# Score tiles in two PSUM slots, probability tiles in a slot of their own, and the order of the work in a step

## What the kernel computes

```python
k_eff = (W_dq.T @ W_uq.T @ W_uk).reshape(nh, hs, n_kvl)
v_eff = jnp.transpose((W_uv.T @ W_o.T).reshape(n_kvl, nh, hs), (1, 0, 2))
c_kv = x @ W_dkv.T
q = (x @ W_dq.T @ W_uq.T).reshape(B, T, nh, hs)
q_lat = jnp.einsum('bqhd,hdl->bhql', q, k_eff)
attn = jnp.einsum('bhql,bkl->bhqk', q_lat, c_kv) / sqrt(hs)
attn = jax.nn.softmax(jnp.where(causal[None, None], attn, -jnp.inf), axis=-1)
y = jnp.einsum('bhql,hld->bqhd', jnp.einsum('bhqk,bkl->bhql', attn, c_kv), v_eff)
x = _layernorm(x + y.reshape(B, T, C))
gate, up = fp4_linear(x, w_gate), fp4_linear(x, w_up)
x = _layernorm(x + fp4_linear(jax.nn.silu(gate) * up, w_down))
```

## Time and profile before

| | |
|---|---|
| median of 3 runs | 754.0 us (752.06 to 757.2) |
| profiled execution | 758.44 us, its span 756.6 us |
| PE busy | 563.6 us, 74% of the span |
| DVE busy | 532.3 us, 70% |
| ACT busy | 412.3 us, 54% |
| POOL busy | 316.0 us, 42% |
| granted TensorE clock, mean | 0.876 of full speed |

### The profile page before, as it was taken

One profiled execution on the slowest core, in us unless ns is written; L12 is line 12 of the kernel. 1 busy time (PEld: TensorE's weight loads), 2 busy tenths in 40 slices (PEclk: granted clock), 3 DMA queues, 4 the chain that ended last, 5 costly groups with the idle time before them and its releaser, 6 DMA issues.

```text
span 756.6 us, 15168 instructions
## 1 busy us (share of the span) xinstructions
PE 563.6 (74%) x5863; PEld 254.3 (34%) x5863; DVE 532.3 (70%) x981; ACT 412.3 (54%) x598; POOL 316.0 (42%) x441
## 2 busy tenths in 40 slices
PE   4275988589787888788888889696978897862623
PEld 2132333233333434333333334242323342421412
DVE  0389787388889767788788778888787784264461
ACT  2311766377665766565576666564656675742220
POOL 4520032000436654433337464533273536258682
PEclk9655999799998999999898999998899998995565
DMA  3393006602300192020300480203000000000000
GB/s 101 77 241 101 2 3 151 145 2 51 94 5 12 31 210 56 15 52 16 92 16 2 90 196 11 56 10 78 3 16 3 3 2 16 1 15 0 0 14 15
DMA packets 34222, 37.91 MB, mean 50 GB/s; under 512 B 6390, under 2 KB 19766, under 8 KB 34150
## 3 DMA queue, kind: packets, MB, share of 16 engines
q1 hardware_dynamic: 33238, 36.39, 20.0%
q10 hardware_dynamic: 912, 0.54, 0.3%
HBM read 19.64 MB, written 16.78 MB: 48 GB/s over the span
## 4 chain that ended last, share of the span: by engine, by line
PE 39%; DVE 31%; POOL 13%; issue 10%; ACT 4%; DMA 2%; SPq 1%; POOLq 0%; DVEq 0%; ACTq 0%
DVE top L837 19%; PE yt_ps L556 11%; PE ring L537 6%; PE ring L520 5%; PE misc L495 3%; PE ring L507 2%; PE misc L466 2%; POOL eg L1151 2%; POOL hx L1123 2%; POOL hx L1121 2%; POOL hx L1125 1%; DVE z L906 1%; PE misc L455 1%; PE misc L486 1%; DVE hc L963 1%
## 5 line engine op out<-in xcount | busy, mean ns | idle before, releaser
L837 DVE TENSOR_REDUCE top<-ring 128x2 f32<-128x1024 f32 (+3 forms) x384 | 349.6, 948 | 113.4 <-PE ring L507 80.2
L715 ACT ACTIVATE probs<-ring 128x1024 f32<-128x1024 f32 x288 | 293.8, 1027 | 132.1 <-PE ring L507 79.7
L556 PE MATMUL yt_ps<-probs,v_op 128*32 128x512 f32 (+3 forms) x1536 | 171.6, 520 | 0.5 <-ACT probs L715 0.5
L537 PE MATMUL ring<-q_op,k_op 59*128 59x512 bf16 (+3 forms) x768 | 124.0, 346 | 50.2 <-DVE top L837 40.3
L520 PE MATMUL ring<-k_op,q_op 56*128 56x512 f16 (+3 forms) x768 | 127.8, 355 | 44.5 <-ACT probs L715 18.9
L520 PEld LDWEIGHTS ring<-k_op,q_op 56*128 56x128 bf16 x768 | 38.4, 96 | 171.0 <-issue 116.8
L1144 POOL TENSOR_TENSOR r<-r,yq 128x128 f32<-128x128 f32 x32 | 14.6, 457 | 168.3 <-DVE yq L876 168.3
L537 PEld LDWEIGHTS ring<-q_op,k_op 59*128 59x128 f16 x768 | 37.7, 95 | 120.8 <-DVE top L837 58.7
L507 PE MATMUL ring<-ident,mask_s 64*128 64x64 bf16 x1024 | 59.5, 198 | 0.0
L507 PEld LDWEIGHTS ring<-ident,mask_s 64*128 64x128 bf16 x1024 | 47.7, 102 | 17.7 <-issue 5.0
L507 PEld LDWEIGHTS ring<-ident,mask_t 64*128 64x128 bf16 x1024 | 47.2, 100 | 18.2 <-issue 6.8
(11 more groups left out here) (170 smaller groups left out, 758.4 us busy)
## 6 DMA issues: line engine op xcount, KB each, us to landing
q_op<-scratch_q SPq DMA_DIRECT2D x32, 224.0 KB
k_op<-scratch_k SPq DMA_DIRECT2D x32, 224.0 KB
scratch_k<-k_part SPq DMA_DIRECT2D x32, 192.0 KB, 3.3
scratch_q<-q_part SPq DMA_DIRECT2D x32, 128.0 KB, 3.1
scratch_q<-q_part SPq DMA_DIRECT2D x16, 192.0 KB, 3.3
xp<-in_L_attn_x_dram SPq DMA_DIRECT2D x4, 512.0 KB, 4.4
r<-in_L_attn_x_dram SPq DMA_DIRECT2D x8, 256.0 KB, 2.8
out_dram<-z SPq DMA_DIRECT2D x8, 256.0 KB, 2.3
```

The lines of the kernel that those rows point to most:

```text
L537: last = nc.tensor.matmul(ring[slot][:, e, at:at + n], k_op[lo:lo + rows, pair, j * P:(j + 1) * P], q_op[lo:lo + rows, pair, (c + 1) * CHU ...
L556: last = nc.tensor.matmul(yt_ps[32 * q:32 * (q + 1), lo:CHUNK], v_op[:, j, 4 * a + q, :], probs[:, (STEPS * a + tile) % P_RING, q % 2, at: ...
L715: nc.scalar.activation(probs[:, n % P_RING, :, :], ring[(2 * n + 1) % 3][:, :, :], ACT.Exp, scale=SCALE).then_inc(t_exp.sem, 1)
L837: last = nc.vector.tensor_reduce(top[:, kc, :, p, i], ring[slot][:, :, at:at + n], AX.X, ALU.max)
```

## The change

Slots 0 and 1 now hold first-pass tiles alone, in turn, and slot 2 holds second-pass tiles alone, until the first-pass tiles run out in the last batch; from there the second pass uses all three. The waits follow: a first-pass tile waits for the maximum of the body two before, a second-pass tile for the exp of the step before. On TensorE the second-pass tile comes right behind the first-pass tile, and the jobs behind both; on ScalarE exp comes first in a step, ahead of the jobs' reads, the k parts and the sigmoid. The 24 tiles ahead of the loop use two slots.

```diff
@@ -317,6 +317,10 @@
 
         block = ctx.enter_context(nc.Block())
 
+        def probs_slot(m):
+
+            return 2 if m < B * BODY - STEPS - LEAD else m % 3
+
         def tile_pos(b, a, s):
 
             u = a + s // STEPS
@@ -578,9 +582,9 @@
                     nc.tensor.transpose(misc[0:w, 0:P], wd[:, f * P:f * P + w], ident[:, :]).then_inc(prep_mm.sem, 1)
 
             for s in range(STEPS + LEAD):
-                if s >= 3:
-                    pe.wait_ge(s_max.sem, s - 2)
-                score_max(0, s // STEPS, s % STEPS, s % 3)
+                if s >= 2:
+                    pe.wait_ge(s_max.sem, s - 1)
+                score_max(0, s // STEPS, s % STEPS, s % 2)
                 if 4 <= s < 4 + 3 * FT:
                     weight_t(s - 4)
                 if s == STEPS + 1:
@@ -598,23 +602,19 @@
                         a, s = n // STEPS, n % STEPS
                         nb, na, ns = tile_pos(b, a, s + STEPS + LEAD)
                         if nb < B:
-                            if n < 2 and b == 0:
-                                pe.wait_ge(s_max.sem, STEPS + LEAD)
-                            else:
-                                pn = b * BODY + n - 2
-                                pe.wait_ge(t_exp.sem, pn + 1)
-                            score_max(nb, na, ns, 2 * n % 3)
-                    for job in jobs_at(b, n):
-                        misc_job(*job)
+                            pe.wait_ge(s_max.sem, b * BODY + n + STEPS + LEAD - 1)
+                            score_max(nb, na, ns, n % 2)
                     if b < B:
 
                         if nb < B:
-                            pe.wait_ge(s_max.sem, b * BODY + n + STEPS + LEAD)
+                            if b * BODY + n > 0:
+                                pe.wait_ge(t_exp.sem, b * BODY + n)
                         else:
                             pe.wait_ge(s_max.sem, B * BODY)
                             pe.wait_ge(t_exp.sem, b * BODY + n - 2)
-                        score_probs(b, a, s, (2 * n + 1) % 3)
-
+                        score_probs(b, a, s, probs_slot(b * BODY + n))
+                    for job in jobs_at(b, n):
+                        misc_job(*job)
                     for w, at in enumerate(W_STEP):
                         g = n - at
                         if g % STEPS == 0 and g >= 0 and b < B:
@@ -712,7 +712,7 @@
                 if g >= 0:
 
                     act.wait_ge(av_mm.sem, g // STEPS * WS + FREED[g % STEPS])
-                nc.scalar.activation(probs[:, n % P_RING, :, :], ring[(2 * n + 1) % 3][:, :, :],
+                nc.scalar.activation(probs[:, n % P_RING, :, :], ring[probs_slot(b * BODY + n)][:, :, :],
                                      ACT.Exp, scale=SCALE).then_inc(t_exp.sem, 1)
 
             def sigmoid(b, t):
@@ -772,6 +772,8 @@
             for b in range(B + 1):
                 for n in range(BODY):
                     a, s = n // STEPS, n % STEPS
+                    if b < B:
+                        exps(b, a, s)
                     for job in jobs_at(b, n):
                         misc_read(*job)
                     if n in K_PART_AT and b + 1 < B:
@@ -779,9 +781,6 @@
                     if b > 0:
                         for stage, t in tile_at(b, n, H_A if b < B else TAIL_H_A):
                             sigmoid(b - 1, t)
-                    if b < B:
-                        exps(b, a, s)
-
                     if s == 7 and b < B:
                         out_copy(b, NC * a)
                     if s == 1:
@@ -859,7 +858,7 @@
             dve.wait_ge(wq_v.sem, 3)
             nc.vector.tensor_scalar(w_b[:, :, :], w_b[:, :, :], 1.0, ROUND, ALU.max, ALU.mult).then_inc(wq_v.sem, 1)
             for s in range(STEPS + LEAD):
-                maximum(0, s // STEPS, s % STEPS, s % 3)
+                maximum(0, s // STEPS, s % STEPS, s % 2)
                 if s == STEPS - 1:
                     combine(0, 0)
 
@@ -991,7 +990,7 @@
                     if b < B:
                         nb, na, ns = tile_pos(b, a, s + STEPS + LEAD)
                         if nb < B:
-                            maximum(nb, na, ns, 2 * n % 3)
+                            maximum(nb, na, ns, n % 2)
                             if ns == STEPS - 1:
                                 combine(nb, na)
                     for kind, jb, k in jobs_at(b, n):
```

## The result

The changed kernel takes **778.5 us** (median of 4 runs, 775.57 to 780.17), the kernel before, in the same session, 755.6 us (4 runs, 752.06 to 760.12). The ratio is 1.0299, 95% interval 1.0261 to 1.0337: 22.6 us slower, where +11 was forecast. The profiled execution took 780.17 us, span 778.2, mean granted clock 0.867; the one before 758.44, 756.6 and 0.876.

A forecast was written before the change was run, and what follows sets the result against it. TensorE was held back by T waiting for max (40.3 us) and S for exp (18.9). Batch terms 6.5 + 1.5 + 3.0 + 0 gave +11 us: 769 on the profiled execution, 765 against the 754.0 median; range 742 to 787.

The forecast's parts named there:

- Batch 0: +6.5: Batch 0: +2.4 us from T_0 to T_25, nothing in steps 25 to 35, +4.1 from T_36 to the end.
- "+1.5" for batch 1: Batch 1: same sum as batch 2's +3.0 us, half given back for one long wait for max before T_36.
- "-1.0" for steps 63 to 71: Batch 2, steps 63 to 71: VectorE full, TensorE gets a tile and its value matmuls ahead, gaining about 1.0 us.
- I take the loss of its first 48 steps and this gain as equal: Batch 3: first 48 steps' loss equals the last 24 steps' gain with three slots for T; sum 0.
- steps 25 to 35 neither gain nor lose: Batch 0, after the last q part is split: SP's queue sets 25.3 us whatever TensorE does; change 0.
- the second sigmoid chain gives 1.1 back: Batch 2, steps 36 to 53: a saving of 1.1 us at the second sigmoid chain, within a term of +1.1.
- T_18 is now ahead, which gives 1.0 back: Batch 2, steps 11 to 17: T_18 no longer behind the q job waiting for up_product; saves 1.0 us, term +0.7.
- +0.5: Batch 2, steps 0 to 10: TensorE's jobs fill most rounds; 24.5 us against 24.02 before.
- rival (1): The forecast: single slot's round binds in lean steps and outweighs what is freed; 765 us, own range 757 to 778, 50%.
- (2): Not slower: freeing T from waiting for max decides, where VectorE has long lists in batches 1 to 3; 736 us, 16%.
- (3): Losses and gains cancel: rounds overlap with work better, or stall chains give back more; 748 to 757 us, 28%.
- (4): TensorE's clock falls to 1.2 GHz in batch 0's lean quads from short idling; about 830 us, 6%.

The follow-up runs named there:

- the slots alone: Kernel before with only the changed slots and waits, its own order kept on TensorE and ScalarE: 779.4 us, ratio 1.0309.
- the short exp: Exp cut to 256 of 512 columns from step 6 of each batch: changed kernel 746.0 us, kernel before 752.1 us.
- batches 1 and 2 changed: Kernel before, its order kept, with the changed slots in batches 1 and 2 alone: 9.8 us slower (5.1 to 14.5).
- the order only: Kernel before with only the changed order on TensorE and ScalarE, three shared slots and waits kept: 763.4 us, ratio 1.0075.

## Why the prediction was off by half

**The mechanism was right.** A single slot closes the round T, exp, T at 1.50 us, and it binds: shown by the slots alone (+23.3) and by the short exp (31 us off the changed kernel, 4 off the other). The forms were right too: 1.50 to 1.51, 1.56 to 1.57 and 1.62 to 1.63 us in lean steps, 29.95 us for the quad where 30.4 was forecast and 27.20 stood before.

**What failed is the size of the sum.** "Batch 0: +6.5" measured 8.2 by itself, "+3.0 for batch 2" 4.3 and "0" for batch 3 2.6, each with the forecast inside its interval or at its edge. Batches 1 and 2 together, forecast at +4.5, measured 9.8 (5.1 to 14.5): that term is too low clear of the noise. "+1.5" for batch 1 is 5.5 as the difference of two kernels of one session; its place isn't shown, for in the trace of batches 1 and 2 changed, steps 11 to 62 of batch 1 took 118.59 us for 119.34. The terms are too low by 9.6 us together, and some 3 more (no more than the intervals allow) came with all batches changed. I counted losses and then set gains against them. These did not come, or were paid for elsewhere:

- "-1.0" for steps 63 to 71: TensorE did gain 3.2 us there, and paid 6.0 in the eleven steps behind, since VectorE's list has to be done first.
- "I take the loss of its first 48 steps and this gain as equal" for batch 3: steps 11 to 47 lost 3.8 us (84.46 for 80.63), and steps 48 to 70, with three slots for T, gained nothing (35.35 for 35.15).
- "steps 25 to 35 neither gain nor lose" in batch 0: SP's queue did hold them at its length (25.8 us from its first write at 121.74 to T_36, 25.3 before), but it starts later. With q's job and its read behind T and exp, the first write comes 2.9 us behind T_25, for 0.8 before, and the stretch takes 28.69 us for 26.13. With slots only it takes 26.55, with the order only 28.49.
- "the second sigmoid chain gives 1.1 back": steps 49 and 50 of batch 2 took 4.11 + 1.60 us before and 4.66 + 3.70 after. Not all of that is the change: in batch 1 of the same trace of before they took 4.46 + 2.73. In the rows below GpSimd's clamp feeds the sigmoid, exp_49 stands behind it on ScalarE, T_50 waits 2.34 us for exp_49, and the next T is at half clock.

```profile
491.69 1.09 POOL L1150 TENSOR_SCALAR eg<-eg 128x352 f32<-128x352 f32 x1
...
493.84 1.01 ACT L715 ACTIVATE probs<-ring 128x1024 f32<-128x1024 f32 x1
...
494.90 0.39 PE L541 MATMUL ring<-q_op,k_op 59*128 59x512 bf16 x2 [2.34 <-ACT probs L715]
...
498.60 0.53 PE L541 MATMUL ring<-q_op,k_op 59*128 59x384 bf16 x2
```

- "T_18 is now ahead, which gives 1.0 back": T_18 starts at 414.36, and steps 11 to 17 are 5.1 us shorter, but the q job behind it waits 3.57 us for up_product, and S_19 and T_19 are stuck behind the q job, at half clock, and steps 18 to 35 are 6.3 us longer. Together steps 11 to 35 lost 1.2 us where +1.9 was forecast: the picture was wrong here and the sum was not too low.

```profile
418.37 2.08 PE L455 MATMUL misc<-x_t,aq 128*128 128x512 f32 x2 [3.57 <-DVE gu L938]
...
421.60 0.62 PE L541 MATMUL ring<-q_op,k_op 59*128 59x512 bf16 x2
```

- Steps 0 to 10, "+0.5": the sum took the larger of work and round and left out where the wait for VectorE would fall. With the half clock behind it the stretch got 6.0 longer, 2.8 net of the steps before the boundary. The two terms of a boundary, -0.5 together, measured +0.2, +2.8 and +1.8.

**The rest, point by point.** Steps 54 to 62, forecast 15.3, took 14.83. Start and end: 0 forecast, -1.3 and +0.4 measured. The wait of k_range for kf, forecast as 0.8 us twice a batch, came in batch 0 (0.61 and 0.79 us) and not in batches 1 and 2, where k_range waited for nothing. A quad has 8 plain tiles, 4 with one mask and 6 cut ones, not 8, 5 and 5; the floor of 28.0 us is the same. Of the order I said that it costs some of the terms; on top of the slots it costs nothing that was measured in the whole time. With 778.5 us the result lies at the top of the 757 to 778 that rival (1) had for itself.

**The rivals.** (2), not slower, fell: the 40.3 us of T on max went, and the waits came back as exp, 19.3, 14.5, 14.1 and 10.7 us of them in batches 0 to 3. (3) fell with it. (4), the clock falling in lean quads, is refuted: the quad ran at 1.00 with TensorE busy for 24.01 of 29.95 us. Where the clock did matter is behind single waits of 2.3 to 3.6 us, a term that no case of mine had. "No T waits for max any more" was right but for that one wait.

## What to carry to other kernels

A buffer of one slot turns producer, consumer and release into a serial round; compare that round with the mean step of the loop, and if it is longer, the loss is there even in stretches that look full of other work. A gain in front of a list that must be done anyway is no gain, so cut stretches behind the list and not in front of it. Before changing who waits, look for instructions on the bound engine that take longer in one place than in another: moving the four instructions of z, 3.12 us for 1.11 to 1.27, gained 0.75% where the whole rearrangement lost 3%.

## What was not expected of the hardware

- Four VectorE instructions z from SBUF to SBUF take 1.11 us, and 3.12 us while GpSimd runs xq products of 1.27 and 1.26 us beside them; singly they take 0.33 to 1.42 us there. Moving them, out of the list as well, gave 0.75% of the time. The maxima, which read PSUM, keep their 1.22 us beside the same products. The Trainium skill, SBUF — State Buffer, section SBUF: two separate sides, says that VectorE and GpSimd share a pair of ports, which the GpSimd instruction, or a VectorE instruction in a two-port mode or with two SBUF inputs, holds for the whole instruction; the rows agree, though none shows in which mode z ran.
- TensorE waited for exp in the quad from step 39 of batch 0, up to 0.90 us at a time, eleven times in 29.95 us, and the clock stayed at 1.00.
- Taking the two heads of T apart cost 41 us of TensorE time with the same matmuls.
